# A window's feature transfer moved behind the window load in one DMA queue

## What is computed

```python
q, k, v = x @ Wq + bq, x @ Wk + bk, x @ Wv + bv        # 3 heads of 128
e = edge_attr @ We + be
alpha = (q[dst] * (k[src] + e)).sum(-1) / sqrt(128)
w = softmax of alpha over the edges of one target
out = segment_sum((v[src] + e) * w, dst).mean(heads) + x @ Ws + bs
h = relu(out + residual)
```

## Time and profile before

| | us |
|---|---|
| median of 3 runs | 3927.33 |
| lowest and highest | 3911.86, 3940.19 |
| span of the profiled execution | 3925.3 |
| its mean granted TensorE clock, as a share of 2.4 GHz | 0.922 |

### The profile page before, as it was taken

The page is one execution under the profiler, slowest core; times in us unless marked ns, Lnnn a source line. Parts: engine busy times, 40 slices in busy tenths (PEclk is TensorE's granted clock), DMA queues, the critical chain, the costliest instruction groups (busy, mean ns, idle before and its releaser), DMA issues. The chain is left out here.

```text
span 3925.3 us, 81257 instructions
## 1 busy us (share of the span) xinstructions
PE 3393.5 (86%) x22381; PEld 2072.9 (53%) x22381; DVE 1826.2 (47%) x5337; ACT 1453.8 (37%) x3467; POOL 1781.0 (45%) x1807
## 2 busy tenths in 40 slices
PE   4999999994875999999699989679888879999998
PEld 1566666662553555655355545345454535555554
DVE  4566666665854444453344444334444332353222
ACT  3555555552243454544233333223333331132122
POOL 1444444551015777774677777377777600000000
PEclk8988889996987999999889998789999989999999
DMA  3566666664836566665778787487777644543133
GB/s 116 170 186 192 187 184 185 178 177 80 255 116 176 157 183 176 184 178 133 201 208 223 217 229 200 118 228 208 203 205 207 164 151 171 177 153 109 55 116 123
DMA packets 717221, 675.09 MB, mean 172 GB/s; under 512 B 383123, under 2 KB 543738, under 8 KB 716810
## 3 DMA queue, kind: packets, MB, share of 16 engines
q1 hardware_dynamic: 623290, 466.05, 40.5%
q0 software_dynamic: 77008, 200.24, 18.9%
q10 hardware_dynamic: 16768, 6.91, 0.7%
HBM read 530.63 MB, written 142.28 MB: 171 GB/s over the span
## 5 line engine op out<-in xcount | busy, mean ns | idle before, releaser
L2190 POOL DMA_INDIRECT l_y<-s_lrows,l_src x1332 | 1331.9, 1000 | 456.7 <-issue 383.7
L3193 PE MATMUL ps<-nl_adj,nl_table 126*128 126x504 bf16 (+1 forms) x3150 | 631.2, 357 | 2.3 <-DVE nl_table L3428 2.3
L951 POOL DMA_INDIRECT em_gs<-s_rows,em_idx x400 | 389.6, 974 | 424.6 <-DMA em_idx<-in_sd 312.4
L3193 PEld LDWEIGHTS ps<-nl_adj,nl_table 126*128 126x128 bf16 x3150 | 301.8, 96 | 298.7 <-issue 5.0
L2230 PE MATMUL ps<-ident,l_y 128*128 128x128 f32 x1800 | 268.0, 285 | 205.7 <-DMA l_y<-s_lrows,l_src 124.1
L2273 PE MATMUL ps<-l_y,aw_pT 128*63 128x277 f32 x2700 | 384.8, 423 | 2.5 <-ACT aw_pT L2467 2.0
L2584 DVE TENSOR_TENSOR l_y<-l_y 128x768 f32<-128x768 f32 x225 | 214.0, 951 | 331.5 <-DMA l_y<-s_lrows,l_src 288.2
L2453 ACT ACTIVATE aw_yT<-ps 128x512 f32<-128x512 f32 (+1 forms) x525 | 262.0, 534 | 256.5 <-PE ps L2230 245.9
L2257 PE MATMUL ps<-aw_yT,aw_qt 128*63 128x384 f32 x1800 | 338.4, 499 | 6.9 <-DMA aw_yT<-s_dxT 6.9
L2230 PEld LDWEIGHTS ps<-ident,l_y 128*128 128x128 f32 x1800 | 205.2, 144 | 263.5 <-issue 201.8
L2619 DVE COPY aw_axd<-ps 128x252 f32<-128x252 f32 x225 | 94.6, 420 | 410.0 <-PE ps L2290 392.9
(11 more groups left out here) (375 smaller groups left out, 5872.9 us busy)
## 6 DMA issues: line engine op xcount, KB each, us to landing
nl_adj<-s_adj SPq DMA_DIRECT2D x20, 3100.8 KB
aw_yT<-s_dxT SPq DMA_DIRECT2D x150, 384.0 KB, 4.4
aw_geoS<-s_geoS SPq DMA_DIRECT2D x450, 94.5 KB
nl_adj<-s_adj SPq DMA_DIRECT2D x15, 2325.6 KB
ws_msg<-s_msg SPq DMA_DIRECT2D x75, 384.0 KB, 3.9
s_dxT<-aw_yT SPq DMA_DIRECT2D x75, 384.0 KB, 4.4
aw_qt<-s_qt SPq DMA_DIRECT2D x225, 126.0 KB
s_msg<-em_msg SPq DMA_DIRECT2D x100, 256.0 KB, 2.5
```

The costliest lines, as they stand in the source:

```text
L951: pool.indirect_dma_start(out=gs[:, u, j, :], out_offset=None, in_=d["rows0"], in_offset=bass.IndirectOffsetOnAxis(ap=idx[:, u, 2 * j:2 * ...
L2190: pool.indirect_dma_start(out=y[:, u, j, 0:W], out_offset=None, in_=table, in_offset=bass.IndirectOffsetOnAxis(ap=src[:, u, j:j + 1], axis ...
L3193: m = nc.tensor.matmul(k.ps[:, bank(i, p), 0:cols * WN], source[:, p, q, b, :], adj[:, a % 2, 0:cols, b * WN:(b + 1) * WN], start=b == 0 a ...
```

## The change

In SyncE's turn the load of window w + 4 is issued ahead of the transfer of dx, instead of behind it.

```diff
             def turn(w, u, i):
+                if started(w, 1) and not (isinstance(w, int) and w + U - 1 >= NW):
+                    load(w + U - 1, (u - 1) % U)
                 if l == 0:
                     store_dx(w, u)
                 elif not (isinstance(w, int) and w + 2 >= NW):
                     load_dx(w + 2, (u + 2) % U)
-                if started(w, 1) and not (isinstance(w, int) and w + U - 1 >= NW):
-                    load(w + U - 1, (u - 1) % U)
                 if queries and started(w, U + 3):
```

## The result

The changed kernel takes 3975.6 us (median of 4 runs, 3963.9 to 3989.8) where the kernel before takes 3925.4 (4 runs, 3911.9 to 3940.2): a ratio of 1.0135, 95% interval 1.0106 to 1.0165. It is slower by 1.35% by that ratio and by 50 us between the two medians, where 155 us were forecast. The sign and the places were right, the size was three times too large; the time is just inside the low end of the range that was given, 3975 to 4190 us.

A forecast was written before the change was run, and what follows sets the result against it. TensorE was taken to set layer 0's pace, GpSimd just behind; in layers 1 and 2 TensorE waits for gathered rows. 3925.3 + 60 (stall) + 62 (clock) + 32 (layer 1) + 0 (layer 2) = 4079, stated as 4080 us; range 3975 to 4190.

The forecast's parts named there:

- 5.5 and 2.4, and 110 in all: Layer 0, ScalarE: waits in us for the store by the copies of u = 2 and u = 3, about 110 over 14 chunks.
- the three signs of being wrong: SyncE's queue not late after the change, the blocked copy waiting under 2 us, or the clock staying at 1.00 through it.
- The landing of 4.4 us: Layer 0, SyncE's queue: the store of features takes 4.4 us from issue to landing, read from the trace before.
- 14 x 4.3 = 60: Layer 0, TensorE: one stall of 4.3 us at u = 2 in each of 14 chunks, 60 us.
- The clock in layer 0, 62 us: Layer 0, TensorE: each of 14 stalls brings a clock fall costing 4.4 us, 62 us, bounds 0 and 105.
- The mean of 4.9 us from layers 1 and 2: Layers 1 and 2: 94 us of lost clock over 19 waits for rows of 2.5 us or more, 4.9 us each.
- Layer 1, +32 us: Late features stall TensorE beyond the waits for rows, 10 us, and 5 more clock falls cost 22 us.
- Layer 2, 0: Features at most 2.4 us late a chunk, under 4.8 us of waits for rows: no cost, bounds minus 49 to plus 56.
- the one in which the stalls come and the clock holds (3995 us): Rival: stalls in layers 0 and 1 cost 60 and 10 us without clock falls, 3995 us; chance 0.2.

The follow-up runs named there:

- r3_query_first: Load ahead of the store in layer 0 only, plus the 630 KB store of queries moved ahead of the features' store at u = 0: 4005.4 us beside 3924.6, ratio 1.0186.
- the four unchanged traces: Traces of four kernels whose order in layers 1 and 2 is that of before; layer 1 took 40.2 to 41.2 us a chunk.
- r2_layers12: Load ahead of the load of features in layers 1 and 2 only, layer 0 as in the kernel before: 3940.2 us beside 3923.3, ratio 1.0048.
- r4_lead3: On top of r2_layers12, yT in five slots and features loaded three windows ahead instead of two: 3955.1 us, ratio 1.0073 to the kernel before.
- r3_outputs_early: Kernel before, with a chunk's output products ahead of the turning of the next window's rows in layers 1 and 2: 3899.8 us, ratio 0.993.
- r3_outputs_early_all: Kernel before, with a chunk's output products ahead of the turning of the next window's rows in all three layers: 3897.0 us, ratio 0.9936.
- r4_all_three: The full change plus five yT slots, features loaded three windows ahead and output products first, all layers: 3900.0 us, ratio 0.9945 to the kernel before.

## Why the prediction was right or wrong

**That it is slower, and where: right.** SyncE's queue was late, the store went behind the six loads, the copies of u = 2 and u = 3 were blocked for it, the score products of u = 2 waited for the copy, and that of u = 3 was hidden by the output products. The two copies wait 3.8 and 2.9 us in the chunk shown, 86.2 us in all; 5.5 and 2.4, and 110 in all, were named. In layer 1 L2257 waits for the load of features and L2230 hardly for rows. The loads kept their places and cost nothing. One of the three signs of being wrong that the prediction named came true: in the chunk shown the clock stayed at 1.00 through the stall.

**The landing of 4.4 us: the first step that failed.** The median of the earlier trace rows is of stores of u = 1, and in the kernel before those stand right behind the store of queries. The store that the change makes critical doesn't; the copy that waits for it starts 3.0 us after its issue. The stall is then 1.24 + 0.85 = 2.1 us of idle time in the chunk shown. TensorE's waits for the copy are 26.9 us in the layer, where 14 x 4.3 = 60 were summed. The row was right and was read for the wrong store. r3_query_first shows it from the other side: put the queries ahead, and the copy starts 4.0 to 4.5 us after the issue, the idle time is 3.25 + 0.85 = 4.1 us, and the waits are 51.2 us in the layer.

The Trainium skill ("DMA: Bandwidth & Descriptors", Anatomy of one DMA) gives 2.0 us plus bytes over 436 GB/s for the DMAs of GpSimd's path, an estimate of 2.9 us for this store, which is on SyncE's queue. The prediction set it aside for the trace's 4.4; the trace of the changed kernel has 2.9 as its median. That fit has no term for what stands ahead of a transfer in its queue, which here was worth 1.2 to 1.5 us.

**The clock in layer 0, 62 us: the second step that failed, and the larger one.** It was taken over from waits of 2.5 us and more in layers 1 and 2. With the idle time in pieces of 1.24 and 0.85 us the clock fell 3 times in twelve chunks, for 10 us at half, and one of the three was not at the stall. TensorE is busy for 8.5 us more with the same products over these chunks, so 5 to 9 us are lost there, and 6 to 10 in 14 chunks. The stall was below the size that the price came from, which followed from the first error. But the price was too high by itself as well: where the stall did have its forecast size, a fall cost 2.6 us and came in each of the 14 chunks, some 35 us and not 62. The mean of 4.9 us from layers 1 and 2 mixes short falls with long ones. The long ones, 13.7 or 17.1 us in the clock's record, stood at waits ahead of the output products.

Together, layer 0's chunk grew by 2.47 us, 35 us in 14 chunks, stall and clock in one, where 60 + 62 were summed.

The Trainium skill ("TensorE: Matmul & The Clock Gate", HAM oscillation) has a loop in which each wait for data is followed by a cold start. In layer 0 the trace agrees where the wait was 3.25 us; with two short pieces it mostly doesn't.

**Layer 1, +32 us: the mechanism right, its two terms the wrong way round.** Against the mean of the four unchanged traces (40.61 us) the two with the changed order (42.06 and 42.25) have 1.55 us more a chunk, 19 us over the twelve chunks from window 8 to 67, or 22 in 14. The stall was priced at 10 us and the additional falls at 22. The falls came, 13 and 12 where 7 or 8 were before, just as many as forecast. But they brought no loss: the time at half clock is 51 and 58 us, against a mean of 62 in the unchanged traces, and TensorE is busy for 437 us on average, against 438. The long wait ahead of the output products had gone, and with it the long falls. The waits themselves came out larger: TensorE's idle time is 69 us against 49, which is the 19 us. In the layer as a whole it waits 79 us in the changed kernel for features and rows, against 52 to 61 in the unchanged traces, since late features at other turns were not all taken from the waits for rows. So that 32 were summed and 22 came is in part luck: one term was too small and the other came to nothing.

**Layer 2, 0: right, as far as these traces tell.** Over windows 8 to 67 TensorE waits 71.6 us for rows and features in the changed kernel and 63.4 in r2_layers12, against 61.2 to 70.6 in the four unchanged traces. Layers 1 and 2 together measure +17 us, with 11 to 27 us as the interval of the ratio, where 32 was summed.

**The sum.** 35 us in layer 0 and 17 behind it make 52 us, against 60 + 62 + 32; timed were 50, with 42 to 65 us as the interval of the ratio. Of the rivals, the one in which the stalls come and the clock holds (3995 us) is the nearest; it had the clock nearly right in layer 0 and the stall too large. What the prediction passed over lightly is GpSimd: it said that TensorE sets the pace of layer 0, because it was busy for 551 of 580 us, with GpSimd just behind. The experiments put GpSimd's gathers at least as near to the bound, but they don't separate the two.

**Still open.** Why a store lands 1.2 to 1.5 us later behind the queries is shown as an effect of order, not explained. And what decides the length of a fall wasn't separated. In windows 8 to 67 of all ten traces of the table, every fall of over 6.8 us stood at a wait for rows ahead of the output products, but the wait's length alone doesn't decide: at that place in the kernel before a wait of 2.51 us had a fall of 13.7 us, and one of 4.01 us had one of 3.4.

## What to carry to other kernels

A landing time is the time of one transfer at one place in its queue: before a median is put into a sum, look at which transfers it was taken from, and whether the moved one will stand behind the same neighbour. A price for the clock belongs to waits of the size and at the place it was read from: the same kind of wait cost up to 17 us at half clock ahead of the output products and at most 6.8 elsewhere. So reordering can make waits cheap without shortening them, as with the output products first, or, as with the earlier load here, gather them at the worst place. And count the slow stretches between the same windows in every kernel: a fall just behind a layer's end, counted in, hides such a gain.

## What the runs showed of the hardware

- A store of the same size, from the same queue, landed in 2.9 us (median) behind loads and in 4.4 us (median) right behind the 630 KB store of queries.
- Layer 0, twelve chunks. Idle in pieces of 1.24 and 0.85 us a chunk: 3 falls of the granted clock, each 3.4 us at half. In pieces of mostly 2.8 to 3.4 and 0.85 us: 12 falls, 5.1 us on average.
- Layer 1, waits of 2.5 to 4.0 us ahead of the output products, in before and r4_lead3 from 1945 to 2500 us: 21 falls, of which 17 last 13.7 or 17.1 us and four 3.4 or 6.8. With the output products moved ahead of the waits (r3_outputs_early, r3_outputs_early_all, r4_all_three), none over 6.8 in windows 8 to 67 of any layer.
- Two traces of the same code differed by up to 12 us in the length of one layer, and by 47 us in its time at half clock, while the whole runs of the kernel before stay within 0.6% of their median.
